# A two-layer decoder on one core: the bank for key and query projections joins the ring of score banks

## The reference

```python
x = ln(x + self_attention(x))           # 16 heads of 8, rotary on q and k          SELF0
x = ln(x + cross_attention(x, ctx))     # 16 heads of 8                             CROSS0
x = ln(x + mixture(x))                  # 8 experts, top 2, all computed, /8        MIX0
x = ln(x + causal_attention(x))         # one head of 128                           CAUSAL1
x = ln(x + cross_attention(x, ctx))     # 16 heads of 8                             CROSS1
x = ln(x + routed_experts(x))           # top 1 of 8, capacity 128                  ROUTE and the end
```

## Time and profile before

| what | value |
|---|---|
| median of 3 runs | 458.1 us (455.65 to 461.03) |
| the profiled execution's own time | 458.44 us |
| its span in the trace | 456.6 us, 9057 instructions |
| PE busy, share of the span | 393.9 us, 86% |
| DVE busy, share of the span | 280.7 us, 61% |
| ACT busy, share of the span | 242.2 us, 53% |
| mean granted clock of TensorE | 0.95 |

### The profile page before, as it was taken

The page is one execution under the profiler, slowest core; times in us unless marked ns, Lnnn a source line. Parts: engine busy times, 40 slices in busy tenths (PEclk is TensorE's granted clock), DMA queues, the critical chain, the costliest instruction groups (busy, mean ns, idle before and its releaser), DMA issues.

```text
span 456.6 us, 9057 instructions
## 1 busy us (share of the span) xinstructions
PE 393.9 (86%) x3284; PEld 337.0 (74%) x3284; DVE 280.7 (61%) x829; ACT 242.2 (53%) x551; POOL 48.1 (11%) x57
## 2 busy tenths in 40 slices
PE   1589999899999999999979999999999698874292
PEld 1577778687778998889968989878898576643292
DVE  2477887978874547732676554685543983934444
ACT  2226567676676654676447566576573265451141
POOL 6200000940000000000000000000001020020115
PEclk9969999999999999999979999999999899996597
DMA  7605311031512000002001002000002002650300
GB/s 270 186 23 143 91 24 42 6 90 31 165 45 47 1 2 1 1 3 46 2 6 41 2 1 47 2 1 1 1 2 59 0 12 71 186 172 0 102 13 31
DMA packets 18907, 22.53 MB, mean 49 GB/s; under 512 B 2984, under 2 KB 13361, under 8 KB 18864
## 3 DMA queue, kind: packets, MB, share of 16 engines
q1 hardware_dynamic: 17344, 18.68, 15.1%
q10 hardware_dynamic: 1008, 2.31, 1.5%
q0 software_dynamic: 512, 0.97, 0.7%
HBM read 13.63 MB, written 2.11 MB: 34 GB/s over the span
## 4 chain that ended last, share of the span: by engine, by line
PE 74%; DVE 14%; issue 5%; ACT 3%; DMA 1%; POOL 0%; POOLq 0%; SPq 0%; DVEq 0%; ACTq 0%
PE bank_D L812 13%; PE bank_C L703 10%; PE bank_D L677 9%; PE bank_A L688 9%; DVE negmax L1190 4%; PE bank_A L828 4%; PE bank_A L830 3%; PE bank_A L829 3%; PE bank_A L619 3%; PE bank_K L599 3%; PE bank_A L620 2%; PE bank_A L1484 2%; PE bank_D L663 2%; PE bank_D L732 1%; PE bank_A L742 1%
## 5 line engine op out<-in xcount | busy, mean ns | idle before, releaser
L1190 DVE TENSOR_REDUCE negmax<-bank_D 128x2 f32<-128x512 f32 x192 | 127.2, 685 | 33.9 <-PE bank_D L677 33.6
L964 ACT ACTIVATE expo<-bank_A 128x512 f32<-128x512 f32 x192 | 110.8, 597 | 46.5 <-PE bank_A L688 44.6
L677 PE MATMUL bank_D<-k_head,q_sp 128*128 128x256 f32 x384 | 93.3, 331 | 5.0 <-DVE negmax L1190 2.5
L1000 ACT ACTIVATE hidden<-bank_A,b 128x256 f32<-128x256 f32 x128 | 53.7, 471 | 59.4 <-PE bank_A L830 59.3
L688 PE MATMUL bank_A<-q_sp,k_head 128*128 128x256 f32 x384 | 81.4, 297 | 1.9 <-DVE q_sp L1185 1.5
L677 PEld LDWEIGHTS bank_D<-k_head,q_sp 128*128 128x128 f32 x384 | 61.8, 199 | 20.2 <-issue 9.5
L812 PE MATMUL bank_D<-mix_w,hidden 128*128 128x128 f32 x512 | 69.4, 278 | 1.1 <-DVE ctx_n L1117 1.1
L812 PEld LDWEIGHTS bank_D<-mix_w,hidden 128*128 128x128 f32 x512 | 62.3, 191 | 7.2 <-issue 5.8
L688 PEld LDWEIGHTS bank_A<-q_sp,k_head 128*128 128x128 f32 x384 | 60.0, 193 | 5.4 <-DVE q_sp L1185 2.9
L703 PE MATMUL bank_C<-expo,v_aug 128*32 128x256 f32 x768 | 51.4, 385 | 1.9 <-ACT expo L964 1.7
L1249 DVE SCALAR_TENSOR_TENSOR y_mixture<-bank_D,g_w,y_mixture 128x128 f32<-128x128 f32 x64 | 22.4, 350 | 45.7 <-PE bank_D L812 45.6
(11 more groups left out here) (180 smaller groups left out, 534.2 us busy)
## 6 DMA issues: line engine op xcount, KB each, us to landing
k_head<-k_sp SPq DMA_DIRECT2D x96, 64.0 KB, 2.0
mix_w<-in_mix_w SPq DMA_DIRECT2D x24, 256.0 KB, 3.2
expo<-in_mix_w SPq DMA_DIRECT2D x6, 256.0 KB, 3.6
proj_w<-in_proj ACTq DMA_DIRECT2D x1, 640.0 KB, 11.4
xe_scratch<-empty_row SPq DMA_DIRECT2D x1, 520.0 KB, 5.2
expo<-xe_scratch SPq DMA_DIRECT2D x2, 260.0 KB, 3.4
expo<-in_spread SPq DMA_DIRECT2D x1, 512.0 KB, 7.9
expo<-in_spread ACTq DMA_DIRECT2D x1, 512.0 KB, 8.5
```

The costliest lines, as they stand in the source:

```text
L677: last = mm(where(seq, b, ("max", k))[:, qt * SEQ:(qt + 1) * SEQ], q_sps[SET[seq, b]][:, k // 4, qt * P:(qt + 1) * P], k_heads[SET[seq, b] ...
L964: activate(expos[SET[seq, b]][:, h % ESLOTS, :], where(seq, b, ("exp", h))[:], ACT.Exp, scale=float(HD) ** -0.5).then_inc(free(seq, b, ("e ...
L1000: last = activate(hidden[:, (e % 2) * FC + f, :], where(seq, b, ("up", n))[:, i * SEQ:(i + 1) * SEQ], ACT.Relu, bias=b1[:, e * FC + f:e * ...
L1190: V.tensor_reduce(negmaxes[SET[seq, b]][:, s // 4, :, 32 * (s % 4)], where(seq, b, ("max", s))[:].rearrange("p (q n) -> p q n", q=QT), AX. ...
```

## The change

Pool K is gone. Pool D has four banks instead of three, and the turns "k" and "q" take the next bank of D like the others. Nothing else in the kernel is edited:

```diff
@@ bank_turns, attention
             if s == KEYS_AT:
-                turn(seq, b, "k", "K")
+                turn(seq, b, "k", "D")
...
             if s == QUERIES_AT:
-                turn(seq, b, "q", "K")
+                turn(seq, b, "q", "D")
@@
-POOLS = {"D": 3, "A": 3, "C": 1, "K": 1}
+POOLS = {"D": 4, "A": 3, "C": 1}
```

## The result

| | before | after |
|---|---|---|
| median of 20 runs | 459.72 us (455.65 to 462.55) | 455.03 us (452.95 to 457.22) |
| ratio, 95% interval | 1 | 0.9906 [0.9888, 0.9925] |
| the profiled execution's own time | 458.44 us | 455.72 us |
| its span | 456.6 us | 453.9 us |

The change is faster by 0.9%. In the batches of the experiments the ratios leave out runs of a slower state (five of the kernel before, one of e5), which the medians there include.

What follows compares the result with a forecast made beforehand. PE was taken to bound the middle (240 to 352 us), with DVE pacing as much near the end. Removing 7.2 us and adding 3.0 gave 4.2 less than 458.44, so 454.2 us; range 450.5 to 460.

Steps and rivals of the forecast that it cites:

- its own sign: Trace after: the sum would be wrong if the clock's falls differ in number or length, the mark of rival 3.
- Waits behind "back": Three stops of L812 and one of L677 after L1117 reads a bank late: all go, 2.8 us removed.
- the wait at 302.16: PE's wait at 302.16 us, its fourth turn read 1.3 us before: counted whole, 0.5 us removed.
- The wait at 231.46: Head 7's wait of 1.69 us passes to the keys' fill right behind it; only 0.3 us gained.
- Short waits: 30 more D fills between 44 and 352 us, 4.0 us in sum: half taken, 2.0 us, bounds 0 and 4.0.
- The held banks: Cross-stage keys or queries hold banks until L1088; four later fills wait, 3.0 us added, bounds 1.5 and 6.
- The first stage: After six reductions in a row, the next stage's keys fill one reduction earlier: 0.6 us removed.
- Rival 3: 220 to 240 us: the clock's fall stays out, up to 3.4 us of matmul time back, 450 to 451 us; 13%.
- The routing of sequence 2: L887 near 368 us can start earlier, and DVE's later idle at L1282 makes that count in full: 1.0 us.
- what was counted at nothing: D waits between 22 and 27 us and most between 354 and 402, where DVE hardly pauses: no gain.
- Rival 1: DVE gives nothing back: PE's lead is lost at the next needed result, 3 to 4 us removed, 457.5 to 458.5; 25%.
- Rival 2: Banks held through L1088 in 16 cross projections cost more than the ring gives: slower, 466 us; 10%.

Runs made afterwards that it cites:

- e5: Kernel before with its old banks; only DVE's reader of keys and queries (L1088) moved into the matmul's tick: 459.94 us, ratio 1.0041.
- e3: Changed kernel with L1088, DVE's reader of keys and queries in the cross stages, in the matmul's tick instead of one later: 452.68 us, ratio 0.9848.
- e10: Repeat of e3, the changed kernel with L1088 in the matmul's tick: 453.28 us, ratio to before 0.9877.
- e9: The changed kernel run again, unaltered, against the kernel before: 455.94 us, ratio 0.9927.
- e2: Changed kernel's four banks in turn only up to head 0 of (1, SELF0), then the old three and one: 457.21 us, ratio to before 0.9945.
- e12: As e2, but four banks in turn only until head 8 of the first stage, then the old banks: 458.49 us, ratio to before 0.9986.
- e8: Against the kernel before: D has four banks to itself, keys and queries take turns in pool A's three: 463.2 us, ratio 1.0119.
- e6: As e3, but with the old three and one banks from head 0 of (2, CROSS1) on: 453.20 us, ratio to before 0.9904.
- e1: Old three and one banks up to head 0 of (1, SELF0), then four in turn as in the changed kernel: 456.29 us, ratio to before 0.9943.
- e4: Against the kernel before: keys and queries join the D ring, which stays at three banks, one bank unused: 466.59 us, ratio 1.0144.

## Why the prediction was right, by its steps

The time forecast, 454.2 us, lies 0.8 us under the median measured, and the 4.2 us less that it rests on compare with 4.3 by the ratio. The steps did less well than their sum: two errors of 2.3 us cancel, and that they do is luck. By its own sign, falls of the clock that differ in number or length, the sum was disturbed: before has recorded falls of 6.8, 3.4, 6.8 and 3.4 us up to 400 us, after 6.8, 6.8 and 3.4, beside the stretch up to about 26 us that its record doesn't hold.

- **Waits behind "back"**, 2.8 us: 2.83 in the ledger, all four without a stop. "I count all of it" failed for one: 1.23 us were gained at 175.84, and at 178.95 PE waited 1.23 us for ACT to drain a bank of pool A, which cost 1.39. No D bank is in that wait. The same befell **the wait at 302.16** (0.5 predicted, 0.62 gained, 0.66 given back at L842). The working looked for the next wait of D banks and of x, and not for those of pool A, which PE reaches sooner too.
- **The wait at 231.46** went as said, the whole of it to the keys behind it: 1.69 gained, 1.77 lost, where 0.3 of gain was booked. The reader that ends the wait came 3.13 us earlier (231.41 to 228.28), and the keys 3.37. So the gain between the two starts is there, 0.24, but PE had come there with a lead of 3.46, 0.35 of it won at L663 just before (229.19), and it lost the difference to DVE here.
- **Short waits**, 2.0 with bounds 0 and 4.0: 2.7 by difference, which also holds whatever else moved. The halving was argued from waits of L688 close behind. The shift does go up by 0.05 to 0.11 us at L688, L619 or L792 shortly behind a good many of these fills, but by some 0.9 us in all, less than half; and the lists have L742 and L688 grow by 0.8 us only up to 352 us.
- **The held banks**, 3.0 us at four places: 2.59 at the same four and nowhere else. The queries of (0, CROSS0) and (1, CROSS0) cost 0.28 each, the keys of (3, CROSS0) 1.46. Only (0, CROSS1) came out smaller, 0.57 for 0.94. e3 and e10 confirm the sum by taking it away: 2.7 us between e9 and e10.
- **The first stage**, 0.6 us, was the term most mis-sized: 2.92 us in the trace of after, 1.4 to 3.0 from head 0 on in all traces that start with four banks, and 2.5 us by e2's times against 0.6 by e12's. At equal clock the runs give 0.4, but at another place than the working had it: at the fill of 37.30 us, which it didn't count, and not at the keys. It didn't look at the clock of that stretch, where 10.1 of 24 us stood at 1.2 GHz. Rival 3's mechanism came true here, and not at its own place: 220 to 240 us shows 0.83 as before. That the fourth bank causes the better clock is not shown, but nine traces with it, e8 among them, have 0 to 6.8 us of recorded falls there, and four of the five with three D banks have 10.2 (e5 has 6.8); six of the nine have no fall near 31 us, and all five have one. Recorded falls leave out the first microseconds. e12 doesn't bear out that its gain reaches the end.
- **The routing of sequence 2**, 1.0 us, and what was counted at nothing behind 354 us. L887 does follow the matmul before it without a stop, and the wait of L848 ahead of it (1.35 in e6's row) went too. But the stretch from 353 to 401 us loses 1.26 us on balance, because the lead met the mask from ACT, then matmuls at 1.2 GHz. "DVE later idles 1.03 us for PE" at L1282 remained, at 1.19:

```profile
369.79 0.61 DVE L1282 SCALAR_TENSOR_TENSOR y_causal<-bank_D,causal_col,x_rows 128x128 f32<-128x128 f32 x2 [1.19 <-PE bank_D L732]
```

So 2.3 us too little at the start stand against 2.3 too much at the end (1.0 and 1.26), and the middle, forecast at 2.6 (0.3, 0.5, 2.8 and 2.0 less 3.0), gave 1.4 in the trace and, with the end, 2.6 in e1's times. Rival 1 describes part of what happened, waits that change their name, but it had only 3 to 4 of the 7.2 us removed, and the ledger has 2.05 us given back to ACT beside some 0.9 in small pieces. Rival 2 needed a mean of 0.45 us for 16 turns; the runs have 2.59 / 16 = 0.16.

## What to carry to other kernels

Before a result of late reading joins a ring of banks, find the fill that comes one ring's length behind it and compare its start with the end of that read. Here that named all four stops and their sum to 0.4 us, and moving the read a tick forward took them away for another 0.5 to 0.6%. A bank is worth its place in the ring whose waits lie on the path: the same bank gave 0.9% in D, and in A, held turns included, nothing. And when a stop is removed, list the next thing that PE needs from every engine, not from the one that the stop was about.

The best kernels here are the change with the remainder written at once, 0.9848 and 0.9877 in its two runs, and the same with the old banks at the end, 0.9904 and 0.9869. The runs don't tell these two apart.

## What the runs showed of the hardware

The granted clock moves from one execution to the next while the order of instructions is the same. After and e9 are one kernel: from 20 to 44 us the first is at 1.2 GHz up to about 26 us, the second from 25.5 us for 3.4 us. The fall of 6.8 us near 230 us is in most traces, is 3.4 us long in e12, and is absent in e2, e4 and e5, although e2 has before's banks there; its absence goes with 1.7 us of shift in e2 (-2.04 at 232 us to -3.71 at 250). That is a third of the whole effect measured here, so a single profiled execution can't weigh such a change. The falls in these stretches are 3.4 or 6.8 us long.

A mean clock of 1.00 in the windows doesn't say that all matmuls ran at 2.4 GHz. The record shows changes, and the kernel's first microseconds have none. The timeline of after, PE near 20 us and at 31 us:

```profile
20.56 0.41 PE L619 MATMUL bank_A<-qk_hi,spread 128*128 128x256 f32 x1
20.78 0.41 PE L620 MATMUL bank_A<-qk_lo,spread 128*128 128x256 f32 x1
...
30.82 0.28 PE L619 MATMUL bank_A<-qk_hi,spread 128*128 128x256 f32 x1
30.94 0.28 PE L620 MATMUL bank_A<-qk_lo,spread 128*128 128x256 f32 x1
```

Start to start it is 0.22 us in the first pair and 0.12 in the second, and the window of 20 to 44 us that holds both says 1.00. In this execution the matmuls of 1.2 GHz reach on to about 26 us, and none follow before 230 us. The kernel of e9, the same, is at 2.4 GHz at 20 us and falls at 25.5. The Trainium skill, TensorE: Matmul & The Clock Gate, section Part 1: The HAM clock gate, says that the throttled state is the default and activity releases it; these rows agree with that.
